# GpSimd DRAINs between the loops of every expert, and transposes inside the first product of the last block, in an attention and mixture-of-experts block

## The chip, the cores and the metric

One Trainium2 chip, one of its cores. The metric is the device time of one execution in microseconds; lower is better. The engines are TensorE (PE, with its weight loads as PEld), VectorE (DVE), ScalarE (ACT), GpSimd (POOL) and SyncE (SP). Each has its own queue of instructions, and they tell each other of progress over semaphores.

## What is computed

The reference, cut to what matters here, for 4096 tokens of 256 features:

```python
h = _layernorm(x, axis=-1) * (1 + ca) + sa
x = x + ga * _L0_attn_ref(h, w_qkv, w_out, b_out)      # linear attention, 16 heads of 64
h = _layernorm(x, axis=-1) * (1 + cb) + sb
x = x + gb * _L0_ffn_ref(h, Wg, bg, W1, b1, W2, b2)

def _L0_ffn_ref(x, Wg, bg, W1, b1, W2, b2):            # 8 experts, 2 per token, hidden size 1024
    gate_probs = jax.nn.softmax(x @ Wg + bg, axis=-1)
    _, top_idx = jax.lax.top_k(gate_probs, k)
    selected = gate_probs * expert_mask                 # expert_mask: one-hot of top_idx, summed
    selected = selected / (selected.sum(-1, keepdims=True) + 1e-08)
    h = jax.nn.gelu(jnp.einsum('bsf,efh->bseh', x, W1) + b1)
    expert_out = jnp.einsum('bseh,ehf->bsef', h, W2) + b2[None, None]
    return jnp.einsum('bsef,bse->bsf', expert_out, selected)
```

## The kernel before

The first half of the span is the attention and the routing: x1, the result of the attention, is written to `out` and, with each token's weights, to the DRAM tensor `xrows`; a list of token numbers per expert is made in `ids`. The change touches the second half, the experts.

Each expert's list is worked off in blocks of rows. `three` wide blocks of 3 x 128 rows come first, then `two` narrow ones of 2 x 128; both counts are read from registers, so each is a loop (`Fori`) on every engine. With the inputs here there are 29 blocks with 68 units of 128 rows, 10 wide and 19 narrow; the last expert has one of each, and its narrow block is the last of the program. `gv` counts the blocks. All products are made in three terms, with a high and a low part of each operand.

What each engine does in block gv:

- GpSimd. `gather` (lines 600 to 610): waits until TensorE has transposed the rows of block gv + 1 (`s_bt`), copies list entries to `gid` (line 605), and issues one indirect DMA per unit that brings rows of block gv + 2 to `listed` (line 609). `rows_of` (612 to 617): waits until all earlier scatters have landed (`s_added`) and copies the row numbers to `y_id` (616). `scatter` (619 to 626): per unit waits for VectorE's `y` and issues an indirect DMA that adds it to `out` (624). The order is gather, rows_of, scatter; in the last expert's narrow block it is rows_of, gather, scatter (lines 656 to 658).
- TensorE. `first` (1726 to 1741): 8 chunks m of the hidden layer into PSUM, 6 matmuls each. `second(gv, size, i, chunks)` (1743 to 1755): row block i of the output, 3 matmuls for each chunk of the hidden layer. `block_T(gv + 1)` (1706 to 1714): the transposes of the next block's rows, 2 per unit. It waits for VectorE's normalization (`s_norm`) and gives `s_bt`.
- ScalarE. For each of four pairs of chunks two gelus to `hid` (879) and a copy to `hid_hi` (883), then `xT_full` of the next block from the transposes (852).
- VectorE. Copies the weights to `y_w` (1403), then for each pair k `hid_lo` (1414); ahead of k = 2 it runs `take` for the next block (1350 to 1355), which waits until that block's rows have landed (`s_rows`), copies their weights to `y_next` (1353) and normalizes two units (1347); ahead of k = 3 `take_third`. Then `xT_hi` and `xT_lo` of the next block, and `y` of each row block (1425, 1426) when TensorE has given it.

At the end of the program VectorE waits for the last scatters to land and tells SP. A block ends (line 89, where the program's code stands in a context) with a DRAIN on every engine and a barrier of them all. The program's code begins with a DRAIN on every engine too (line 1802).

Of the kernel before, what the change touches and what calls it, by code (L numbers as in the profile page):

```python
# [29 lines left out]
M = FH // P  # L30
# [9 lines left out]
BI = BT // P  # L40
# [46 lines left out]
def adaln_block(nc, x, w_qkv, w_out, b_out, Wg, bg, W1, b1, W2, b2, cvec, wmod, out):  # L87
    ctx = ExitStack()
    with ctx:
# [32 lines left out]
        units = sb("units", [P, E], I32)  # L122
# [210 lines left out]
        s_blo = sem("s_blo")  # L333
# [172 lines left out]
        def _(pool):  # L506
# [125 lines left out]
            def expert(e, par, three, two, last):  # L632

                nb = three + two
                pool.reg_mov(to, e * COLS)

                def ahead(j):

                    over = j // nb
                    col = e * COLS + 2 * j + three  # L640
                    if last:
                        pool.reg_mov(at, col * (1 - over))
                    else:
                        pool.reg_mov(at, col + over * (COLS - 2 * nb - three) + j // (nb + 1))
                    return pool.snap(at, min_val=0, max_val=E * COLS - 1)

                with pool.Fori(0, three) as b:
                    gv = now(pool, g)
                    gather(ahead(b + 2), gv + 2)
                    rows_of(pool.snap(to, min_val=0, max_val=E * COLS - 3), gv, 3)  # L650
                    scatter(gv, 3)
                    pool.reg_add(to, to, 3)
                    pool.reg_add(g, g, 1)
                with pool.Fori(0, two) as b:
                    gv = now(pool, g)
                    if last:
                        rows_of(pool.snap(to, min_val=0, max_val=E * COLS - 2), gv, 2)
                        gather(ahead(three + b + 2), gv + 2, 2)
                    else:
                        gather(ahead(three + b + 2), gv + 2)  # L660
                        rows_of(pool.snap(to, min_val=0, max_val=E * COLS - 2), gv, 2)
                    scatter(gv, 2)
                    pool.reg_add(to, to, 2)
                    pool.reg_add(g, g, 1)
# [236 lines left out]
        def _(dve):  # L901
# [484 lines left out]
            def expert(e, par, three, two, last_expert):  # L1386

                def w_low_part(n):

                    dve.wait_ge(s_whi, now(dve, w) * 4 + (n + 1 + FOUR))  # L1390
                    if n < 2:
                        return dve.tensor_tensor(w1_lo[1 - par][:, n, :], w1_raw[:, n, :], w1_hi[1 - par][:, n, :].bitcast(F32), ALU.subtract)
                    m = slice((n - 2) * 4, (n - 2) * 4 + 4)
                    return dve.tensor_tensor(w2_lo[1 - par][:, m, :], w2_raw[:, m, :], w2_hi[1 - par][:, m, :].bitcast(F32), ALU.subtract)

                def rows_block(size, parts):
                    T = size * P
                    units = size if last_expert else BI
                    chain.begin()
                    gv = now(dve, g)  # L1400
                    dve.wait_ge(s_meta, gv + (1 + ONE))
                    dve.wait_ge(s_y, gv * 3 + THREE)
                    link(dve.tensor_copy(y_w[:, :, :], y_next[:, :, :]))
                    if parts:
                        w_low_part(0)
                        w_low_part(1)
                    for k in range(M // 2):
                        if k == 2:
                            take(gv + 1, units)
                        if k == 3 and units == BI:  # L1410
                            take_third()
                        dve.wait_ge(s_hidhi, gv * 4 + (k + 1))
                        m = slice(2 * k, 2 * k + 2)
                        dve.tensor_tensor(hid_lo[:, m, 0:T], hid[:, m, 0:T], hid_hi[:, m, 0:T].bitcast(F32), ALU.subtract).then_inc(s_hid, 1)  # L1414

                    if parts:
                        w_low_part(2)
                    block_parts(gv + 1, units)
                    dve.wait_ge(s_added, now(dve, wide_u if size == 3 else narrow_u) * 16 + DMA3)

                    def rows_out(i):
                        dve.wait_ge(s_f2, gv * 3 + (i + 1 + THREE))
                        bank = Y2 if i == 2 else Y0 + i
                        slot = i if size == 3 else BI + i
                        link(dve.tensor_tensor(y[:, slot, :], ps[:, bank, 0:D], b2_bc[:, e, :], ALU.add))
                        dve.scalar_tensor_tensor(y[:, slot, :], y[:, slot, :], y_w[:, i, e:e + 1], gates[:, 1, :], ALU.mult, ALU.mult).then_inc(s_y, 1 if i < size - 1 else BI - i)

                    rows_out(0)
                    if parts:
                        w_low_part(3).then_inc(s_wlo, 1)  # L1430
                        dve.reg_add(w, w, 1)
                    for i in range(1, size):
                        rows_out(i)
                    chain.end()
                    dve.reg_add(g, g, 1)
                    dve.reg_add(u, u, size)
                    dve.reg_add(got, got, units)
                    dve.reg_mov(wide_u if size == 3 else narrow_u, u)

                with dve.Fori(0, three) as b:  # L1440
                    rows_block(3, not last_expert)
                if not last_expert:
                    dve.memset(tick[:, :], 0.0).then_inc(s_wfree, 1)
                with dve.Fori(0, two) as b:
                    rows_block(2, False)
# [8 lines left out]
        def _(pe):  # L1454
# [268 lines left out]

            def expert(e, par, three, two, last_expert):

                def first(gv, size):

                    T = size * P
                    pe.wait_ge(s_blo, gv + 1)
                    for m in range(M):  # L1730
                        k = m // 2
                        if size == 3 and m in (4, 6):
                            pe.wait_ge(s_gelu, gv * 4 + (k - 1 + FOUR))
                        if m == (3 if size == 3 else 6):
                            pe.wait_ge(s_y, gv * 3 + THREE)
                        to = ps[:, k, (m % 2) * T:(m % 2 + 1) * T] if size == 2 else ps[:, m % 4, 0:T]
                        col = slice(m * P, (m + 1) * P)
                        for w_, a, st, sp_ in three_terms([((w1_hi[par][:, c, col], w1_lo[par][:, c, col]), (xT_hi[:, c, 0:T], xT_lo[:, c, 0:T])) for c in range(C)]):
                            last = pe.matmul(to, w_, a, start=st, stop=sp_)  # L1739
                        if m % 2:  # L1740
                            last.then_inc(s_f1, 1)

                def second(gv, size, i, chunks):

                    bank = Y2 if i == 2 else Y0 + i
                    if 0 in chunks and i == 2:
                        pe.wait_ge(s_gelu, gv * 4 + (M // 2 + FOUR))
                    r = slice(i * P, (i + 1) * P)
                    for m in chunks:
                        if i == 0 and m % 2 == 0:  # L1750
                            pe.wait_ge(s_hid, gv * 4 + (m // 2 + 1 + FOUR))
                        for a, w_, st, sp_ in three_terms([((hid_hi[:, m, r], hid_lo[:, m, r]), (w2_hi[par][:, m, :], w2_lo[par][:, m, :]))]):
                            last = pe.matmul(ps[:, bank, 0:D], a, w_, start=m == 0 and st, stop=m == M - 1 and sp_)  # L1753
                    if M - 1 in chunks:
                        last.then_inc(s_f2, 1 if i < size - 1 else BI - i)
# [3 lines left out]
                most, end = range(0, M - 2), range(M - 2, M)  # L1759
                with pe.Fori(0, three) as b:  # L1760
                    gv = now(pe, g)
# [9 lines left out]
                    pe.reg_add(w, w, 1)  # L1771
                with pe.Fori(0, two) as b:
                    gv = now(pe, g)
                    first(gv, 2)
                    if last_expert:
                        second(gv, 2, 0, range(0, 2))
                        block_T(gv + 1, 2)
                        second(gv, 2, 0, range(2, M))
                        second(gv, 2, 1, range(0, M))
                    else:  # L1780
                        second(gv, 2, 0, most)
                        block_T(gv + 1)
                        second(gv, 2, 1, most)
                        second(gv, 2, 0, end)
                        second(gv, 2, 1, end)
                    pe.reg_add(g, g, 1)
# [26 lines left out]
```

## Time and profile before

| | |
|---|---|
| time, median of 3 runs | 803.26 us (802.91 to 805.48) |
| time of the profiled execution | 803.23 us |
| its span, first to last instruction | 801.1 us |
| TensorE busy | 752.4 us (94%) |
| VectorE busy | 606.2 us (76%) |
| ScalarE busy | 461.5 us (58%) |
| GpSimd busy | 338.6 us (42%) |
| mean granted TensorE clock | 0.976 |

Busy times overlap and don't add up to the span. The chain that ended last is found by going back from the last instruction to what released it; what is on it sets the time. DRAINs, waits, branches and register instructions are not counted as busy. The profiled interval of an indirect DMA on GpSimd is its issue; when it has landed is told by who waits for it.

### The profile page before, as it was taken

How to read it: one execution, taken by the hardware profiler on the slowest of the kernel's cores; microseconds unless marked ns; L12 is line 12 of the kernel's file. 1: busy time of each engine (PE TensorE's matmuls, PEld its weight loads, DVE VectorE, ACT ScalarE, POOL GpSimd, SP SyncE). 2: the span in 40 equal slices, each digit the busy share in tenths (PEclk: the TensorE clock that was granted, in tenths of full speed). 3: DMA queues.
4: the chain of work that ended last, by engine and by line, in shares of the span. 5: the costliest groups of instructions: out<-in, count | busy, mean ns of one | idle time of the engine just before them, and what ended most of it. 6: DMA issues, size and time to landing. Idle time of an engine off the chain costs nothing.

```text
span 801.1 us, 16804 instructions
## 1 busy us (share of the span) xinstructions
PE 752.4 (94%) x5846; PEld 686.2 (86%) x5846; DVE 606.2 (76%) x1328; ACT 461.5 (58%) x841; POOL 338.6 (42%) x291
## 2 busy tenths in 40 slices
PE   4979999999999999976699999999999999999995
PEld 4767778788888789963599999999999999999994
DVE  6899999988898755799577767676676876876653
ACT  4465555656654542359557667574666666765643
POOL 2441413423322102400256564646556565565554
PEclk9999999999999999985799999999999999999998
DMA  8500000000000135580253532626325235233323
GB/s 286 169 1 1 1 1 1 2 1 2 1 1 2 53 106 173 171 228 5 94 146 65 145 64 42 170 43 167 54 61 145 55 83 123 49 49 60 51 56 47
DMA packets 45602, 59.58 MB, mean 74 GB/s; under 512 B 8002, under 2 KB 38788, under 8 KB 45412
## 3 DMA queue, kind: packets, MB, share of 16 engines
q0 software_dynamic: 14352, 21.85, 15.0%
q1 hardware_dynamic: 31188, 36.93, 14.5%
q8 instruction: 36, 0.59, 0.3%
q14 instruction: 26, 0.21, 0.1%
HBM read 40.49 MB, written 18.27 MB: 73 GB/s over the span
## 4 chain that ended last, share of the span: by engine, by line
PE 74%; DVE 16%; issue 5%; ACT 2%; DMA 1%; POOL 1%; POOLq 0%; DVEq 0%; SPq 0%; ACTq 0%
PE ps L1739 23%; PE ps L1753 23%; PE ps L1539 7%; PE ps L1497 7%; PE ps L1564 3%; PE ps L1713 2%; PE ps L1548 2%; PE ps L1636 2%; DVE q_max L966 2%; DVE q_sum L973 2%; DVE k_blk L1076 2%; DVE q_exp L967 1%; ACT at_lo L814 1%; DVE ln_s L930 1%; PE ps L1618 1%
## 5 line engine op out<-in xcount | busy, mean ns | idle before, releaser
L879 ACT ACTIVATE hid<-ps,b_col 128x256 f32<-128x256 f32 (+1 forms) x232 | 105.6, 507 | 113.9 <-PE ps L1739 111.0
L1753 PE MATMUL ps<-w_hi,hid_hi 128*128 128x256 f32 x544 | 154.4, 284 | 0.0
L1753 PE MATMUL ps<-w_hi,hid_lo 128*128 128x256 f32 x544 | 151.9, 279 | 0.0
L1753 PE MATMUL ps<-w_lo,hid_hi 128*128 128x256 f32 x544 | 151.9, 279 | 0.0
L1414 DVE TENSOR_TENSOR hid_lo<-hid,hid_hi 128x512 fp32r<-128x512 f32 (+1 forms) x116 | 90.9, 784 | 73.4 <-ACT hid_hi L883 73.3
L1739 PE MATMUL ps<-xT_hi,w_hi 128*128 128x256 f32 (+1 forms) x464 | 139.6, 301 | 1.6 <-DVE xT_lo L1366 1.6
L1739 PE MATMUL ps<-xT_lo,w_hi 128*128 128x256 f32 (+1 forms) x464 | 139.5, 301 | 0.0
L1739 PE MATMUL ps<-xT_hi,w_lo 128*128 128x256 f32 (+1 forms) x464 | 139.4, 300 | 0.0
L624 POOL DMA_INDIRECT out<-y,y_id x68 | 117.3, 1725 | 39.5 <-POOL y_id L616 16.6
L545 POOL TENSOR_TENSOR q_n<-q_exp,q_rec 128x1024 f32<-128x1024 f32 (+1 forms) x33 | 61.0, 1851 | 172.5 <-DVE q_rec L974 172.5
L609 POOL DMA_INDIRECT listed<-xrows,gid x86 | 94.2, 1096 | 42.0 <-POOL gid L605 24.6
L1753 PEld LDWEIGHTS ps<-w_hi,hid_hi 128*128 128x128 f32 x544 | 102.3, 188 | 0.0
L1753 PEld LDWEIGHTS ps<-w_lo,hid_hi 128*128 128x128 f32 x544 | 102.3, 188 | 0.0
L1753 PEld LDWEIGHTS ps<-w_hi,hid_lo 128*128 128x128 f32 x544 | 102.2, 188 | 0.0
L1497 PE MATMUL ps<-wqk_hi,h_q 128*128 128x512 f32 x248 | 92.6, 416 | 1.6 <-DVE q_exp L967 1.4
L1739 PEld LDWEIGHTS ps<-xT_hi,w_hi 128*128 128x128 f32 x464 | 88.1, 190 | 2.0 <-DVE xT_lo L1366 2.0
L712 ACT ACTIVATE k_exp<-ps,k_new 128x512 f32<-128x512 f32 x64 | 44.0, 687 | 77.8 <-DVE k_new L1077 76.4
L1739 PEld LDWEIGHTS ps<-xT_lo,w_hi 128*128 128x128 f32 x464 | 87.9, 189 | 0.0
L1739 PEld LDWEIGHTS ps<-xT_hi,w_lo 128*128 128x128 f32 x464 | 87.8, 189 | 0.0
L883 ACT ACTIVATE hid_hi<-hid 128x512 fp32r<-128x512 f32 (+1 forms) x116 | 82.0, 707 | 3.7
L1539 PE MATMUL ps<-h_q,wqk_hi 128*128 128x512 f32 x256 | 80.3, 395 | 0.0
L1076 DVE TENSOR_REDUCE k_blk<-ps 128x1 f32<-128x512 f32 x64 | 43.4, 678 | 19.8 <-PE ps L1539 19.4
(215 smaller groups left out, 1454.0 us busy)
## 6 DMA issues: line engine op xcount, KB each, us to landing
w_raw<-in_L_ffn_W SPq DMA_DIRECT2D x16, 1024.0 KB
x_all<-in_L_attn_x SPq DMA_DIRECT2D x8, 512.0 KB, 9.3
out<-x_all SPq DMA_DIRECT2D x8, 512.0 KB, 3.0
xrows<-x_all SPq DMA_DIRECT2D x8, 512.0 KB, 4.5
listed<-xrows,gid POOLq DMA_INDIRECT x86
out<-y,y_id POOLq DMA_INDIRECT x68
wqk_raw<-in_L_attn_w_qkv SPq DMA_DIRECT2D x2, 512.0 KB, 6.4
wqk_raw<-in_L_attn_w_qkv SPq DMA_DIRECT2D x1, 1024.0 KB, 10.5
```

What stands on the lines that cost most here:

```text
L545: ins = pool.tensor_tensor(q_n[:, s % 2, i, :].rearrange("p (h d) -> p h d", d=DH)[:, hs, :], q_exp[:, i % 2, :].rearrange("p (h d) -> p h ...
L609: pool.indirect_dma_start(listed[:, i, :], None, xrows[:, :], bass.IndirectOffsetOnAxis(ap=gid[:, i:i + 1], axis=0)).then_inc(s_rows, 16)
L624: pool.indirect_dma_start(out[:, :], bass.IndirectOffsetOnAxis(ap=y_id[:, i:i + 1], axis=0), y[:, i if size == 3 else BI + i, :], None, co ...
L712: act.activation(k_exp[:, n % 2, :], ps[:, KT + n % 2, :], ACT.Exp, bias=k_new[:, s % 2, j:j + 1]).then_inc(s_ke, 1)
L879: ins = act.activation(hid[:, m, 0:T], src, ACT.Gelu_apprx_tanh, bias=b1_col[:, e, m:m + 1])
L883: act.activation(hid_hi[:, m, 0:T], hid[:, m, 0:T], ACT.Copy).then_inc(s_hidhi, 1)
L1076: link(dve.tensor_reduce(k_blk[:, j:j + 1], ps[:, KT + n % 2, :], AX, ALU.max, negate=True))
L1414: dve.tensor_tensor(hid_lo[:, m, 0:T], hid[:, m, 0:T], hid_hi[:, m, 0:T].bitcast(F32), ALU.subtract).then_inc(s_hid, 1)
L1497: last = pe.matmul(ps[:, b + half, :], a, w, start=st, stop=sp_)
L1539: last = pe.matmul(ps[:, KT + n % 2, :], w, a, start=st, stop=sp_)
L1739: last = pe.matmul(to, w_, a, start=st, stop=sp_)
L1753: last = pe.matmul(ps[:, bank, 0:D], a, w_, start=m == 0 and st, stop=m == M - 1 and sp_)
```

## The change

GpSimd gets a DRAIN behind the loop of wide blocks of each of the eight experts. In the last expert's narrow blocks VectorE takes the next block's rows ahead of the first pair (k = 0) instead of the third, TensorE makes the next block's transposes behind 5 of the 8 chunks of the first product instead of behind 2 chunks of the second, and the second product does 6 chunks of row block 0, 2 of row block 1, the last 2 of row block 0 and the last 6 of row block 1.

```diff
@@ GpSimd, expert
                     scatter(gv, 3)
                     pool.reg_add(to, to, 3)
                     pool.reg_add(g, g, 1)
+                pool.drain()
                 with pool.Fori(0, two) as b:
@@ VectorE, rows_block
                     for k in range(M // 2):
-                        if k == 2:
+                        if k == (2 if units == BI else 0):
                             take(gv + 1, units)
@@ TensorE, expert
-                def first(gv, size):
+                def first(gv, size, ms=range(M)):

                     T = size * P
-                    pe.wait_ge(s_blo, gv + 1)
-                    for m in range(M):
+                    if 0 in ms:
+                        pe.wait_ge(s_blo, gv + 1)
+                    for m in ms:
@@ TensorE, narrow blocks
                     gv = now(pe, g)
-                    first(gv, 2)
                     if last_expert:
-                        second(gv, 2, 0, range(0, 2))
+                        first(gv, 2, range(0, M - 3))
                         block_T(gv + 1, 2)
-                        second(gv, 2, 0, range(2, M))
-                        second(gv, 2, 1, range(0, M))
+                        first(gv, 2, range(M - 3, M))
+                        second(gv, 2, 0, most)
+                        second(gv, 2, 1, range(0, 2))
+                        second(gv, 2, 0, end)
+                        second(gv, 2, 1, range(2, M))
                     else:
+                        first(gv, 2)
                         second(gv, 2, 0, most)
```

`units` is 2 in the last expert's narrow blocks alone, `BI` is 3, `M` is 8, `most` is chunks 0 to 5 and `end` chunks 6 and 7.

In TensorE's queue, before, the end of the first product and the start of the second in the last narrow block (line 1739 is the first product, 1753 the second, 1713 the transposes):

```order
L1739 MATMUL ps<-xT_lo,w_hi 128x256
L1739 MATMUL ps<-xT_hi,w_lo 128x256
L1751 ISA
L1753 MATMUL ps<-w_hi,hid_hi 128x256
L1753 MATMUL ps<-w_lo,hid_hi 128x256
L1753 MATMUL ps<-w_hi,hid_lo 128x256
L1753 MATMUL ps<-w_hi,hid_hi 128x256
L1753 MATMUL ps<-w_lo,hid_hi 128x256
L1753 MATMUL ps<-w_hi,hid_lo 128x256
L1708 ISA
L1713 MATMUL ps<-ident,listed 128x128 x4
```

The transposes stand behind two chunks of the second product. After, the piece around them (lines are up to two higher: 1741, 1714):

```order
L1741 MATMUL ps<-xT_hi,w_hi 128x256
L1741 MATMUL ps<-xT_lo,w_hi 128x256
L1741 MATMUL ps<-xT_hi,w_lo 128x256
L1709 ISA
L1714 MATMUL ps<-ident,listed 128x128 x4
L1741 MATMUL ps<-xT_hi,w_hi 128x256
L1741 MATMUL ps<-xT_lo,w_hi 128x256
L1741 MATMUL ps<-xT_hi,w_lo 128x256
```

They now stand inside the first product, with three of its chunks behind them.

In VectorE's queue, the same block before:

```order
L1403 COPY y_w<-y_next 128x24
L65 REGISTER_ALU
L1412 ISA
L1414 TENSOR_TENSOR hid_lo<-hid,hid_hi 128x2x256
L1412 REGISTER_ALU
L1414 TENSOR_TENSOR hid_lo<-hid,hid_hi 128x2x256
L421 ISA
L1353 COPY y_next<-listed 128x24
L1347 TENSOR_SCALAR listed<-listed 128x256 x2
```

And after:

```order
L1404 COPY y_w<-y_next 128x24
L65 REGISTER_ALU
L421 ISA
L1354 COPY y_next<-listed 128x24
L1348 TENSOR_SCALAR listed<-listed 128x256 x2
L1413 ISA
L1415 TENSOR_TENSOR hid_lo<-hid,hid_hi 128x2x256
```

The take has moved ahead of all four hid_lo. GpSimd's queue is the same but for the DRAINs, which such a listing leaves out.

## Rows read from the trace of the kernel before

**Rows 1.** The page: span, and the chain that ended last, by engine.
```profile
span 801.1 us, 16804 instructions
...
PE 74%; DVE 16%; issue 5%; ACT 2%; DMA 1%; POOL 1%; POOLq 0%; DVEq 0%; SPq 0%; ACTq 0%
```

**Rows 2.** The chain of waits, 490 to 545 us: start us, us, what.
```profile
503.16 5.65 PE ps L1739 x48
508.81 2.12 PE ps L1753 x18
510.93 0.66 PE ps L1713 x6
...
```

**Rows 3.** The chain of waits, 740 us to the end.
```profile
783.48 3.76 DMA out<-y,y_id
...
787.49 0.20 POOL y_id L616
...
793.11 2.64 POOLq L89
```

**Rows 4.** Line 89: engine, operation, ns min/median/max, first and last start us.
```profile
L89 POOLq DRAIN  x1: 7792/7792/7792, 793.1 to 793.1; - x1
...
L89 DVEq DRAIN  x1: 17/17/17, 798.2 to 798.2; - x1
L89 SPq DRAIN  x1: 7/7/7, 798.3 to 798.3; - x1
```

**Rows 5.** GpSimd's timeline, last row: start us, us, engine, line, operation.
```profile
794.18 1.57 POOL L624 DMA_INDIRECT out<-y,y_id  x1 [0.30 <-issue]
```

**Rows 6.** One stretch: busy us of PE, PEld, DVE, ACT, POOL; clock, DMA share, GB/s.
```profile
798.00:799.00 1.00, 0.00 (x0) 0.00 (x0) 0.00 (x0) 0.00 (x0) 0.00 (x0) 0.50 0.00 0
```

**Rows 7.** Line 1802, where the program begins: columns as in rows 4.
```profile
L1802 POOLq DRAIN  x1: 183/183/183, 0.4 to 0.4; - x1
```

**Rows 8.** DMA issues by line: out<-in, queue, operation, count, median us to landing.
```profile
listed<-xrows,gid POOLq DMA_INDIRECT x86
out<-y,y_id POOLq DMA_INDIRECT x68
...
listed<-xrows,ids POOLq DMA_INDIRECT x6, 2.8
```

**Rows 9.** GpSimd's timeline from the third expert's wide to its narrow blocks.
```profile
508.58 1.55 POOL L624 DMA_INDIRECT out<-y,y_id  x1 [0.30 <-DVE y_next L1353]
511.83 0.19 POOL L605 COPY gid<-ids 128x3 int32 x1 [1.70 <-PE ps L1713]
...
515.78 0.96 POOL L609 DMA_INDIRECT listed<-xrows,gid  x1 [0.30 <-issue]
```

**Rows 10.** VectorE's and TensorE's timelines in the narrow block after that.
```profile
519.93 0.17 DVE L1353 COPY y_next<-listed 128x24 f32<-128x24 f32 x1
520.02 0.73 DVE L1347 TENSOR_SCALAR listed<-listed 128x256 f32<-128x256 f32 x2
520.71 0.69 DVE L1414 TENSOR_TENSOR hid_lo<-hid,hid_hi 128x512 fp32r<-128x512 f32 x1
...
521.69 0.28 PE L1753 MATMUL ps<-w_hi,hid_hi 128*128 128x256 f32 x1
```

**Rows 11.** Timelines of GpSimd, VectorE and TensorE around the last block.
```profile
777.34 0.95 POOL L609 DMA_INDIRECT listed<-xrows,gid  x1 [0.30 <-issue]
...
782.49 0.69 DVE L1414 TENSOR_TENSOR hid_lo<-hid,hid_hi 128x512 fp32r<-128x512 f32 x1 [1.58 <-ACT hid_hi L883]
...
786.74 0.69 DVE L1414 TENSOR_TENSOR hid_lo<-hid,hid_hi 128x512 fp32r<-128x512 f32 x1 [0.72 <-ACT hid_hi L883]
...
791.86 0.48 DVE L1426 SCALAR_TENSOR_TENSOR y<-y,y_w,gates 128x256 f32<-128x256 f32 x1
...
785.71 0.60 PE L1713 MATMUL ps<-ident,listed 128*128 128x128 f32 x4
...
787.56 0.31 PE L1753 MATMUL ps<-w_hi,hid_hi 128*128 128x256 f32 x1
```

## The prediction

> **What bounds the kernel now.** Three views, in this order: the page for the whole, the chain of waits for the expert stage and the end, and the answers on single lines for the DRAINs and the last block. The page gives a span of 801.1 us and a chain that is 74% TensorE and 1% GpSimd [rows 1]. In the expert stage that chain holds TensorE alone: first product, second product, transposes, second product, back to back [rows 2]. So an edit on GpSimd or VectorE there costs or gains nothing until TensorE has to wait for it. In the last 18 us the chain leaves TensorE and runs over GpSimd: the third scatter of the wide block lands 3.76 us after its start, at 787.24, the copy to y_id follows at 787.49, then two gathers, two scatters, and line 89 [rows 3]. Line 89 is the end of the block, and there GpSimd has a DRAIN. It starts at 793.1 and lasts 7.792 us, so to 800.9; SP's and VectorE's are over at 798.3 [rows 4]. The last scatter of the program holds GpSimd from 794.18 to 795.75 [rows 5]; with the 3.76 us of [rows 3] it lands at 797.94, and from 798 on the DMA engines are idle [rows 6]. The DRAIN therefore ends 5.15 us after GpSimd's last instruction and 3.0 us after the last landing. As nothing else lasts beyond 798.3, 2.6 us of the span are this DRAIN alone.
>
> **What a DRAIN costs.** Before has two on GpSimd. The one at the start, with no DMA behind it, lasts 183 ns [rows 7]. The one at the end has 160 indirect DMAs behind it (86 + 68 + 6) [rows 8]. Two readings fit both. (i) It goes through the DMAs issued since the last DRAIN one by one: 5.15 us / 160 = 0.032 us each, and it can't end before the last has landed. (ii) It waits for the last landing and then takes a fixed 3.0 us. No row decides; a new DRAIN is bounded by 0.18 us from below and by landing plus 3.0 us from above. I take (i): in the 3 us after the landing there is no transfer that a fixed wait could be for, and with nothing outstanding the price is not paid.
>
> **The DRAINs with more experts behind them, seven of the eight.** The third expert's is typical. The third scatter of its wide block starts at 508.58 and is issued by 510.13; the next copy to gid waits until 511.83 [rows 9] for the transposes, whose piece of the chain ends at 511.59 [rows 2]. The scatter lands at 508.58 + 3.76 = 512.34. A DRAIN that ends there, plus 0.5 us, puts the copy to gid at 512.8, 1.0 us late. The 0.5 us are twice the 0.25 us between landing and copy in [rows 3]: once until the DRAIN's end is noticed, once for branch, registers and waits, which ran ahead before. Queued behind it on GpSimd are three gathers, the last starting at 515.78 [rows 9], a copy to y_id and two scatters. Who waits: VectorE's take in the next block, at 519.93 [rows 10]. With 2.8 us to landing [rows 8] the rows are there at 518.6, 1.35 us ahead. Beyond the take there is 0.3 us more: hid_lo of the third pair ends at 521.40, TensorE wants it at 521.69 [rows 10]. That is 1.6 us of cover against 1.0 us of lateness: cost 0, with 0.6 us left. If the cover is gone, the third hid_lo is late next, then the transposes. By (i) the counting is covered as well: at most about 26 DMAs lie between two DRAINs, 26 x 0.032 = 0.8 us after 510.13.
>
> **The DRAIN in the last expert.** The third scatter lands at 787.24, and the copy to y_id waits for that anyway [rows 3]; the counting of 26 DMAs is over before. Added are the same 0.5 us (bounds 0 and, by (ii), 3.5). Behind it stand everything that ends the kernel, two gathers and two scatters, and they move as a whole: VectorE's last y is done at 792.34 [rows 11], and its scatter starts only at 794.18 [rows 5].
>
> **The DRAIN at the end.** By (i) four DMAs are left to it, it ends with the last landing, and what stands at 798.3 becomes the end: -2.6 us. By (ii) 0.
>
> **Take, transposes and second product in the last expert's narrow block.** There is one such block, the last of the program. TensorE has the same 96 matmuls and 4 transposes in another order. Transposes cost 0.66 us for six [rows 2], so 0.44 us for these four. They now stand ahead of the second half of the third pair instead of behind the second product's first two chunks, so gelu, hid_hi and hid_lo of the last two pairs come 0.44 us later: hid_lo of the fourth ends at 787.87 instead of 787.43 [rows 11]. TensorE wants it after 18 matmuls more than stood ahead of the transposes before (785.71 [rows 11]), at 2.12 us for 18 [rows 2]: 785.71 + 0.44 + 2.12 = 788.27. The two chunks of the second row block that are put in between give that room; before, TensorE's matmul there showed 0.31 instead of 0.28 us [rows 11]. Its end stays where it is. Take now stands in the 1.58 us in which VectorE is idle ahead of the first hid_lo, from 780.91 to 782.49; its rows land at 777.34 + 2.8 to 3.8 = 780.1 to 781.1 [rows 11], and copy and two normalizations take 0.9 us [rows 10], so it ends at 782.0 at the latest. GpSimd's gather in this block stands behind the copy to y_id, so earlier transposes release nothing. Cost 0, under the 1.8 us of cover of the last y. One risk: the fourth hid_lo now runs beside GpSimd's copy to y_id and could stretch it by 0.2 to 0.4 us.
>
> **Sum.** The profiled execution took 803.23 us (span 801.1 and 2.1 around it), the median is 803.26; the sum stands for both. 803.2 + 0 (seven DRAINs) + 0.5 (the eighth) - 2.6 (the end) + 0 (the block) = **801.1 us**. About 0.3%, 2.4 us, is what a measurement of this kernel can tell from no change; the forecast lies just inside that.
>
> **Rivals.** *A DRAIN is light, and the end keeps its tail.* The new ones wait for GpSimd's own instructions, 0.2 us, and what is slow at the end belongs to the end. For it: SP's and VectorE's DRAINs last 7 and 17 ns [rows 4]. Against it: on GpSimd it is the same instruction in both places. Time: 803.2, up to 803.8 with stretched copies. The Trainium skill (VectorE: DVE Perf Modes, "The DRAIN you can't avoid") calls the DRAINs that the runtime puts on all five engines constant, about 12 ns; by that rule this rival holds and the time is 803.2. SP's and VectorE's rows agree with it, GpSimd's 183 and 7792 ns do not.
>
> *A DRAIN is slow every time.* Reading (ii), landing plus 3.0 us. In seven experts the gathers come 4.0 us late against 1.6 us of cover, and TensorE stands 2.4 us each, 16.8 us. In the last expert y_id comes 3.5 us late, and the end keeps its tail. Time: 803.2 + 16.8 + 3.5 = 823.5. It decides from the point where a DRAIN ends more than 0.6 us after the landing. For it: the 3.0 us behind the last landing, which no row ties to a number of DMAs. Against it: a fixed time of that length has no work to be seen in.
>
> *Between them*, a fixed 1 us after each landing: 7 x 0.4 + 1.5 - 2.0 = +2.3, so 805.5.
>
> **How the numbers follow.** DMAs counted one by one (801.1, own range 800.5 to 801.9): 0.57. Light DRAIN: 0.23. Slow: 0.18. Between: 0.02. The range runs from 800.5 (the eighth DRAIN free, 803.2 - 2.6, rounded down) to 804.2 (light DRAINs, copies stretched in every block) and leaves out the last two, 0.20. Faster by over 0.3% needs more than 2.4 us, the lower end of the likeliest case: 0.15. Slower: the last two, 0.20. Same: 0.65.
>
> **What would show it.** Right: ten DRAINs of GpSimd, the eight new ones ending with the landing of the scatter ahead of them; the last ending near 798.6; the last block's copy to y_id near 788.0; TensorE without idle time in the expert stage. Light: the new ones end with the third scatter, and the last still ends 5 us behind GpSimd. Slow: TensorE waits some 2 us in the second narrow block of every expert. The prediction is wrong if TensorE's waits in that stage add up to over 1 us, or if the last DRAIN ends over 1 us after the last landing.

## The result, and the profile after

| | before | changed |
|---|---|---|
| time, median | 803.09 us (801.89 to 805.48, 4 runs) | 830.73 us (828.7 to 832.0, 4 runs) |
| ratio, 95% interval | | 1.034 [1.030, 1.037] |
| span of the profiled execution | 801.1 us | 829.9 us |
| mean granted TensorE clock | 0.976 | 0.959 |

The change costs 27.6 us, where 801.1 us was forecast and 804.2 us was the end of the range. The page of the changed kernel shows at once that the chain is another one. Span and shares of the chain by engine (before: [rows 1]):

```profile
span 829.9 us, 16812 instructions
...
PE 53%; DVE 19%; issue 14%; POOL 4%; POOLq 3%; DMA 3%; ACT 3%; DVEq 0%; SPq 0%; ACTq 0%
```

TensorE's share has gone from 74% to 53%, and POOLq, GpSimd's sequencer with the DRAINs in it, has 3%. The next view is that of TensorE's waits from 390 us to 830 us (what waited, for whom: us in total, times, longest):

```profile
PE ps L1755 <- DVE hid_lo L1415: 19.4, 7, 3.7
PE ps L1741 <- DVE xT_lo L1367: 1.6, 1, 1.6
```

The second line is there before too, with the same 1.6 us; the first is new. Seven times the second product waits for `hid_lo`, once in each of experts 1 to 7: 3.65, 3.41, 3.66, 3.49, 2.60 and 2.28 us, and only 0.3 us in expert 7. The DRAINs, before the narrow loops and at line 89, with their ns (shortest, median, longest; before: [rows 4]):

```profile
L654 POOLq DRAIN  x8: 6610/9928/10841, 411.1 to 811.5; - x8
```

```profile
L89 POOLq DRAIN  x1: 6445/6445/6445, 823.1 to 823.1; - x1
L89 DVEq DRAIN  x1: 17/17/17, 829.6 to 829.6; - x1
L89 SPq DRAIN  x1: 7/7/7, 829.7 to 829.7; - x1
```

The one at the end is over at 829.5, before VectorE's: its tail of 2.6 us is gone, as forecast. The longest of line 654 is the third expert's:

```profile
L654 POOLq DRAIN  x1: 10841/10841/10841, 516.6 to 516.6; - x1
```

A DRAIN stands in its sequencer ahead of its time, beside the scatters that are still being issued (it starts at 516.55, the last scatter before it only at 519.54), so its length is no cost. Its end is: 516.55 + 10.84 = 527.39. GpSimd's timeline there answers to [rows 9]:

```profile
515.36 1.63 POOL L624 DMA_INDIRECT out<-y,y_id  x1 [0.92 <-DVE y L1427]
517.29 1.95 POOL L624 DMA_INDIRECT out<-y,y_id  x1 [0.30 <-issue]
519.54 1.55 POOL L624 DMA_INDIRECT out<-y,y_id  x1 [0.30 <-issue]
528.51 0.19 POOL L605 COPY gid<-ids 128x3 int32 x1 [7.41 <-issue]
529.55 1.03 POOL L609 DMA_INDIRECT listed<-xrows,gid  x1 [0.86 <-POOL gid L605]
```

From the end of the third scatter's issue to the copy to `gid` it is 7.41 us, before 1.70 us [rows 9]: the copy is **5.7 us late**, where 1.0 us was forecast. The chain of waits carries that on to TensorE:

```profile
521.09 6.33 issue
...
530.88 0.98 POOL listed L609
...
532.17 2.80 DMA listed<-xrows,gid
534.97 0.02 issue
534.99 0.06 DVE y_next L1354
...
535.82 0.61 DVE hid_lo L1415
536.42 0.04 issue
536.47 1.65 PE ps L1755 x6
```

The 6.33 us are the DRAIN. Then come the gathers, the landing of the rows (2.80 us), VectorE's take, and behind the take in VectorE's queue the `hid_lo` for which TensorE waits. This is the way that the prediction drew; only TensorE had 3.66 us to wait at its end:

```profile
536.47 0.58 PE L1755 MATMUL ps<-w_hi,hid_hi 128*128 128x256 f32 x1 [3.66 <-DVE hid_lo L1415]
536.85 0.41 PE L1755 MATMUL ps<-w_lo,hid_hi 128*128 128x256 f32 x1
```

And the matmuls behind the wait last 0.41 us in place of 0.28 us. The stretches around it show why (us; busy us of PE, PEld, DVE, ACT, POOL, with the number of instructions; clock, DMA share, GB/s):

```profile
530.00:534.00 4.00, 2.81 (x25) 2.60 (x23) 0.69 (x1) 2.96 (x7) 2.71 (x4) 1.00 0.31 80
534.00:538.00 4.00, 1.53 (x7) 1.53 (x8) 2.35 (x6) 0.00 (x0) 3.31 (x2) 0.73 0.36 55
538.00:542.00 4.00, 4.00 (x21) 4.00 (x20) 1.75 (x4) 2.56 (x4) 1.49 (x2) 0.50 0.29 33
542.00:546.00 4.00, 4.00 (x28) 4.00 (x28) 1.86 (x5) 0.56 (x1) 2.46 (x4) 0.91 0.37 102
```

Before, the same piece of the work ran at full clock, 37 matmuls in 4 us:

```profile
522.00:526.00 4.00, 4.00 (x37) 4.00 (x35) 2.44 (x5) 2.82 (x5) 1.50 (x2) 1.00 0.30 33
```

From about the end of the wait TensorE is granted half its clock, 1.2 GHz, here for 6.8 us (535.9 to 542.7), and from 538 to 542 it does 21 matmuls. The same is seen around the end of four of the other five long waits, for 3.4 or 6.8 us; behind the sixth expert's, 2.28 us long, the clock stays full. Before, the clock is full from 394 to 796 us. The whole stage, after and before:

```profile
390.00:830.00 440.00, 411.90 (x3196) 410.26 (x3195) 277.50 (x555) 250.34 (x441) 234.04 (x215) 0.97 0.36 78
```

```profile
390.00:801.00 411.00, 401.29 (x3196) 401.08 (x3194) 278.12 (x555) 249.86 (x441) 235.94 (x215) 0.99 0.39 83
```

**The books.** The same 3196 matmuls are 10.6 us longer (411.90 − 401.29). With 19.4 us of waits, and 1.2 us less from TensorE's last matmul to the end of the span (8.6 us, before 9.8 us), that makes 28.8 us, and the spans differ by 28.8. The clock accounts for the 10.6 us: the five stretches at half clock are 23.8 us long, 2.4 us of them are still waits, and half of the rest is 10.7 us.

### The profile page after: what moved, and what is told of

Same layout as the page of the kernel before. It is cut to its first block, busy times and chain, and to the rows that moved or that the text cites. A ratio compares the mean times of both kernels' runs of the same rounds, so it can differ in the third digit from the quotient of the medians.

```text
span 829.9 us, 16812 instructions
## 1 busy us (share of the span) xinstructions
PE 764.5 (92%) x5846; PEld 696.6 (84%) x5846; DVE 605.8 (73%) x1328; ACT 461.8 (56%) x841; POOL 336.5 (41%) x291
## 4 chain that ended last, share of the span: by engine, by line
PE 53%; DVE 19%; issue 14%; POOL 4%; POOLq 3%; DMA 3%; ACT 3%; DVEq 0%; SPq 0%; ACTq 0%
PE ps L1741 14%; PE ps L1755 13%; PE ps L1540 7%; PE ps L1498 6%; PE ps L1565 3%; DMA listed<-xrows,gid 2%; PE ps L1549 2%; POOLq L654 2%; PE ps L1637 2%; DVE q_max L967 2%; POOL listed L609 2%; POOL out L624 2%; PE ps L1714 2%; DVE q_sum L974 2%; DVE k_blk L1077 2%
## 5 line engine op out<-in xcount | busy, mean ns | idle before, releaser
L1755 PE MATMUL ps<-w_hi,hid_hi 128*128 128x256 f32 x544 | 158.6, 291 | 19.4 <-DVE hid_lo L1415 19.4
L1755 PE MATMUL ps<-w_lo,hid_hi 128*128 128x256 f32 x544 | 154.6, 284 | 0.0
L1755 PE MATMUL ps<-w_hi,hid_lo 128*128 128x256 f32 x544 | 154.4, 284 | 0.0
L1755 PEld LDWEIGHTS ps<-w_hi,hid_hi 128*128 128x128 f32 x544 | 105.5, 194 | 20.8 <-DVE hid_lo L1415 20.8
L1755 PEld LDWEIGHTS ps<-w_lo,hid_hi 128*128 128x128 f32 x544 | 105.7, 194 | 0.0
L1755 PEld LDWEIGHTS ps<-w_hi,hid_lo 128*128 128x128 f32 x544 | 105.2, 193 | 0.0
L853 ACT ACTIVATE xT_full<-ps,modc 128x384 f32<-128x384 f32 (+1 forms) x58 | 35.4, 660 | 49.5 <-PE ps L1714 49.5
## 6 DMA issues: line engine op xcount, KB each, us to landing
wqk_raw<-in_L_attn_w_qkv SPq DMA_DIRECT2D x1, 1024.0 KB, 10.6
```

The source lines that it names most:

```text
L853: act.activation(xT_full[:, c, 0:units * P], ps[:, XTB + c, 0:units * P], ACT.Identity, bias=modc[:, 2, c:c + 1], scale=modc[:, 3, c:c + 1 ...
```

## Where the 5.7 us came from

The forecast had the third scatter land 2.2 us after its issue (512.34 in before's time). It lands 5.4 us after it, and **it was as late before the change** (5.1 us): by the DMA records in the trace of the kernel before, the scatters that stand ahead of the first narrow block of experts 1 to 6 land 4.4 to 5.35 us after their issue, and those elsewhere 2.1 to 2.6 us. Nobody waited for them there, so no chain showed it. Two views of the kernel before did, and the prediction used neither. The first is SyncE's timeline, the second DMA shares around the scatter at 508.58:

```profile
504.34 0.37 SPq L462 DMA_DIRECT2D w_raw<-in_L_ffn_W  x1
504.75 0.47 SPq L463 DMA_DIRECT2D w_raw<-in_L_ffn_W  x1
```

```profile
508.00:510.00 2.00, 2.00 (x19) 2.00 (x19) 1.99 (x6) 1.94 (x5) 1.70 (x2) 1.00 1.03 329
510.00:512.00 2.00, 2.00 (x20) 2.00 (x20) 0.69 (x1) 0.73 (x2) 0.30 (x2) 1.00 1.11 312
512.00:514.00 2.00, 2.00 (x20) 2.00 (x19) 1.60 (x4) 0.86 (x2) 1.15 (x2) 1.00 1.10 217
514.00:516.00 2.00, 2.00 (x20) 2.00 (x19) 1.66 (x5) 0.00 (x0) 1.39 (x3) 1.00 0.28 72
```

When VectorE is through with an expert's wide blocks, it releases SyncE, which starts the loads of a later expert's weights, two of 1 MB. They fill all DMA engines (a share of 1.03 to 1.11 at 217 to 329 GB/s) until about 514, and the scatter shares them. Each DRAIN stands just behind that scatter. For experts 7 and 8 there is nothing left to load; the changed kernel's wait in expert 7 is 0.3 us, against 2.28 to 3.66 us in the six with a load. It was the scatter of the last expert, with 3.76 us from the start, that the prediction took for all.

So there are three suspects for the lateness: the landing, what the DRAIN does behind it, and the way from the DRAIN's end to the copy. And a rival for the whole: the new order in the last block, or something in the DRAIN beyond the place where it stands.

## The experiments

**1. The DRAINs alone, and the order alone.** The kernel before with each half of the change.

```diff
@@ GpSimd, expert, before's kernel
                     pool.reg_add(g, g, 1)
+                pool.drain()
                 with pool.Fori(0, two) as b:
```

> The eight DRAINs without the new order of the last block. Theory A (the loss is the DRAINs, through TensorE's waits and the clock that they cost): within 1 us of the changed kernel, 830 us, and TensorE waits again some 19 us for hid_lo in seven experts. Rival B (the new order of the last block takes a part of the loss): below 829 by that part. If the order is worth nothing, the two kernels differ by under 1 us.

Measured: 835.2 us (832.7 to 836.2), ratio 1.040 [1.037, 1.042].

```profile
PE ps L1754 <- DVE hid_lo L1415: 21.2, 7, 3.7
```

> The new order of take, transposes and second product in the last block, without DRAINs. Theory A: the end is set by GpSimd, whose chain (landing of the third scatter, y_id, two gathers, two scatters) is untouched, so 803.1 within 0.4 us. Rival B: the order costs time, over 804. A third possibility, a gain, would need GpSimd's last scatter to start earlier than 3.2 us ahead of the last landing, and nothing in the order gives that.

Measured: 803.42 us (801.8 to 805.9), ratio 1.001 [0.999, 1.002], no wait of the second product. Its last DRAIN has its whole tail again:

```profile
L89 POOLq DRAIN  x1: 8180/8180/8180, 791.3 to 791.3; - x1
...
L89 DVEq DRAIN  x1: 17/17/17, 796.8 to 796.8; - x1
```

The DRAINs make all of the loss, and the reordered block by itself costs nothing, as forecast. That the DRAINs alone stand 4.5 us above the whole change, where 1 us was expected at most, raised the question whether the order gives something back.

**2. The changed kernel once more**, unchanged.

> The changed kernel once more, beside the others on one chip, for its difference to the kernel with the DRAINs alone (830.7 and 835.2 in two measurements). If the new order gives 4.5 us back, this is at 830.7 again; if the two differ by the scatter of how long TensorE waits and how the clock answers, it lies anywhere from 829 to 836.

Measured: 831.9 us (827.3 to 835.1), ratio 1.034 [1.031, 1.038]; its profiled execution has a span of 833.0 us and waits of 19.6 us, with 1.6 us more of waits in the DRAINs-only kernel. The profiled spans overlap (829.9 and 833.0 against 832.7). By the medians 3.1 to 4.5 us lie between the two kernels, by the ratios 4.5 to 4.9 us, and no view explains them. In experiments 1 and 6 the order moves nothing; whether it gives something back beside DRAINs between the loops stays open.

**3. DRAINs at two places.** Behind the wide blocks of the second and of the last expert alone.

```diff
@@ GpSimd, expert, before's kernel
                     pool.reg_add(g, g, 1)
+                if e in (1, E - 1):
+                    pool.drain()
                 with pool.Fori(0, two) as b:
```

> DRAINs behind the wide blocks of experts 2 and 8 alone, with about 31 and 128 DMAs behind them. It asks how the time after the landing grows with the number. Straight line through the changed kernel's eight (0.04 us + 0.0425 us each): 1.4 us for the first, 5.5 us for the second. Line with a ceiling near 69 DMAs (as the 2.98 us after 163 DMAs at the end of before would have it): 1.4 and 3.0. Counting alongside from the end of the last issue (0.032 us each): the second ends 4.1 us after the last issue, 1.9 us after the landing. The time: TensorE waits in one expert instead of seven, so about 4 us, and the end gives 2.6 back while the eighth DRAIN costs its 3 to 5.5 us: 807 to 811.

Measured: 807.94 us, ratio 1.006 [1.004, 1.009] (2 runs); TensorE waits once, 3.9 us, in the second expert. The last expert has no load and no wait. So one DRAIN beside a load costs some 5 us, about a seventh of the loss. The second expert's DRAIN, with 31 DMAs behind it, ends 1.32 us after the last landing, as expected (1.4). The last expert's, with 128, ends only 0.71 us after; all three readings of the expectation, 5.5, 3.0 and 1.9 us, were too high.

**4. Small loads.** If the loads make the landing late, DRAINs beside small loads must cost much less. Of the weights of experts 3 to 8 only columns 0 to 7 are loaded (the rest of those experts' weights is left out, and everything else runs as it did), without and with the eight DRAINs.

```diff
@@ SyncE, before's kernel
-                load_weights(e)
+                sp.dma_start(w1_raw[:, :, 0:8], W1[e, :, 0:8].rearrange("(c p) n -> p c n", p=P)).then_inc(s_w1raw, 16)
+                sp.dma_start(w2_raw[:, :, 0:8], W2[e, :, 0:8].rearrange("(m p) n -> p m n", p=P)).then_inc(s_w2raw, 16)
```

> Before, but of the weights of experts 3 to 8 only 8 columns are loaded (24 KB per expert or so instead of 2 MB), so the output of those experts is not the reference's; all matmuls and waits stay. It is the base for the next kernel. TensorE bounds the stage and never waits for weights, so 803 within 1 us.

> The same small loads with the eight DRAINs behind the wide blocks. Theory A says that six of the DRAINs are long because the scatter ahead of them shares the DMA engines with 2 MB of weights (it lands 4.4 to 5.7 us after its issue, against 2.2 in experts 7 and 8). With small loads (experts 3 to 8; the loads of experts 1 and 2 are issued earlier) the landings of all are 2.2 us after the issue, a DRAIN ends 3.1 us after it, the copy to gid comes 4.2 us after it instead of 1.7, 2.5 us late against some 1.6 to 2.0 of cover: TensorE waits 0.5 to 1 us in seven experts, as in expert 7 of the kernel with DRAINs alone (0.84), 4 to 7 us in all, and the clock falls less or not: 806 to 810 against small loads without DRAINs at 803. Rival D (the landing is late because the DRAIN itself holds it up): the landings stay at 5 us and the time at 830 or more.

Measured: 802.58 us without DRAINs, ratio 1.000 [0.999, 1.001], and 809.07 us with them, ratio 1.009 [1.007, 1.011]. Waits of the second product, and the third expert's DRAIN in GpSimd's timeline, in the second kernel:

```profile
PE ps L1755 <- DVE hid_lo L1416: 3.2, 5, 1.2
```

```profile
509.05 1.55 POOL L625 DMA_INDIRECT out<-y,y_id  x1 [0.30 <-issue]
514.79 0.18 POOL L606 COPY gid<-ids 128x3 int32 x1 [4.19 <-issue]
```

The same 21 DMAs stand behind the same DRAIN, and it ends 3.1 us after the issue (with loads 6.3 us). The copy is 4.19 − 1.70 = 2.5 us late, and no wait is over 1.2 us. (The longest is the fourth expert's, where the scatter lands 3.5 us after its issue even so, and not 2.1 to 2.3 as in the others.) So the loads themselves cost nothing (802.58), and the DRAINs beside small ones 6.5 us. Beside full ones they cost 29.0 us in the changed kernel (831.9 against 802.87, same chip) and 32.1 in the DRAINs-only kernel. **22 to 26 us of the loss need the loads.** The remaining 6.5 us also show that the forecast would have been wrong without them: 2.5 us late, not 1.0.

**5. A plain wait in each DRAIN's place.** GpSimd waits there until all earlier scatters have landed, and does nothing else.

```diff
@@ GpSimd, expert, before's kernel
                     pool.reg_add(g, g, 1)
+                pool.wait_ge(s_added, now(pool, u) * 16 + DMA3)
+                pool.sem_inc(s_turn_pool, 1)
                 with pool.Fori(0, two) as b:
```

> Before, with a wait in the place of each DRAIN: GpSimd waits until all scatters up to there have landed, as rows_of does, and goes on. It parts the wait for the landing from the DRAIN's own work (0.7 to 1.1 us behind the landing, and some 1.1 us from its end to the next copy). Theory A: the copy to gid then comes 0.3 us behind the landing, so 5.2 + 0.3 = 5.5 us behind the issue instead of 7.4, 1.9 us earlier; TensorE waits some 1.6 us instead of 3.5 in the experts that load weights, nothing in experts 7 and 8: 10 us of waits instead of 20, and with less of the half clock 812 to 818. If the DRAIN's own work were all of the loss, 803; if none of it, 830. The last DRAIN stays at 3 us behind the landing.

Measured: 827.89 us (826.6 to 828.2), ratio 1.031 [1.029, 1.033]. The expectation was too low by 10 us and more: **the wait for the landing, with the way from there to the copy, brings most of the loss** (25.0 of 29.0 us), with no DRAIN in the kernel but those of before. Its waits, its chain and GpSimd's timeline in the third expert:

```profile
PE ps L1755 <- DVE hid_lo L1416: 16.0, 7, 3.6
```

```profile
517.46 6.79 DMA out<-y,y_id
524.79 0.25 POOLq L644
525.68 0.80 issue
526.47 0.78 POOL listed L609
```

```profile
517.46 1.55 POOL L624 DMA_INDIRECT out<-y,y_id  x1 [0.30 <-issue]
525.44 0.19 POOL L605 COPY gid<-ids 128x3 int32 x1 [6.42 <-issue]
```

The first line of the chain is the number that the prediction needed: 6.79 us from the start of this scatter to its landing, where it had 3.76 [rows 3]. The copy comes 525.44 − 524.25 = 1.2 us after the landing. That is a way behind any halt at this place: the loop's branch, and the registers for the list's position (POOLq L644), which ran ahead before. With a DRAIN it is 0.9 us from landing to the DRAIN's end and 1.1 us from there to the copy. Against the changed kernel it has 3.4 us less of waits (16.0) and 2.3 us less of TensorE's busy time (409.6 us in the stage), but 1.6 us more from TensorE's last matmul to the end (10.2 against 8.6 us), since its last DRAIN has its tail back: 4.1 us in sum. The profiled spans, 829.9 and 825.8 us, are 4.1 us apart, the medians on the same chip 4.0. The DRAINs-only kernel, with this one's order, is 7 us above it (1.040), more by what experiment 2 left unexplained.

**6. The DRAINs behind the narrow loops.** There GpSimd has no work in hand until TensorE's next transposes, and no DRAIN stands in front of a gather that someone needs soon.

```diff
@@ GpSimd, expert
                     pool.reg_add(to, to, 2)
                     pool.reg_add(g, g, 1)
+                if not last:
+                    pool.drain()
```

> Before, with seven DRAINs in another place: behind the loop of narrow blocks of experts 1 to 7, so ahead of the next expert's wide block, where GpSimd is idle for 4.8 us; the last block's order as before. Theory A (a DRAIN ends at the last landing plus about 0.04 us for each DMA since the last DRAIN): the scatter ahead has no weight load beside it and lands some 2.2 us after its issue, 15 to 26 DMAs take 0.7 to 1.2 us, the sequencer 1.1 us more, in all 4.0 to 4.5 us after the issue, against about 4.8 us of idle time. TensorE waits for nothing, and the last DRAIN has 10 DMAs behind it instead of 163, so that it ends with SP's: 803.1 - 2.5 = 800.6 us. Rival C (a DRAIN costs a fixed time that only shows when it is slow, and the end's tail belongs to the end): 803.1 or more, and the last DRAIN still ends 3 us after the last landing.

> The kernel before with a DRAIN behind the narrow loops of experts 1 to 7, once more, beside the run above. If its gain of 2 us is real, 800.2 to 801.5 us, ratio 0.996 to 0.999 with an interval below 1; if it was scatter, 802.5 to 803.5.

> The changed kernel's order in the last block, with the seven DRAINs behind the narrow loops of experts 1 to 7 instead of the eight between the loops. If all of the loss comes from where the DRAINs stand, this is as fast as the kernel before with the moved DRAINs, 800.4 to 801.4 us, with no wait of TensorE over 1 us in the expert stage. If the reordered last block adds something once GpSimd's lists are short, it differs from that kernel by over 0.5 us.

Measured:

| kernel | time, us | ratio to before |
|---|---|---|
| before's order, moved DRAINs | 800.87 (800.1 to 801.7) | 0.9975 [0.9964, 0.9986] |
| the same again | 800.73 (800.3 to 800.9) | 0.9972 [0.9961, 0.9983] |
| the changed kernel's order, moved DRAINs | 800.47 (799.8 to 802.0) | 0.9971 [0.9961, 0.9982] |

Seven DRAINs in the right place make the kernel 2.2 to 2.5 us **faster than before** by the medians, a small gain, but the interval lies below 1 all three times. The last of the three kernels, its DRAINs and GpSimd's timeline across the DRAIN at 530.05:

```profile
L666 POOLq DRAIN  x7: 6017/6263/6564, 436.2 to 765.5; - x7
```

```profile
531.52 1.73 POOL L624 DMA_INDIRECT out<-y,y_id  x1 [0.30 <-issue]
538.12 1.20 POOL L605 COPY gid<-ids 128x3 int32 x1 [4.86 <-PE ps L1715]
```

```profile
L89 POOLq DRAIN  x1: 5787/5787/5787, 793.1 to 793.1; - x1
...
L89 DVEq DRAIN  x1: 17/17/17, 798.7 to 798.7; - x1
```

That DRAIN is over at 530.05 + 6.05 = 536.1, and the copy is still released by TensorE's transposes (PE ps), with the 4.86 us of idle time that it has without any DRAIN. The one at line 89 has 10 DMAs left and ends at 798.9, with VectorE's. From the start of the last scatter to the end of the span it is 4.5 us, before 6.9 us: this is the whole gain. The order of the last block makes no difference here either, 800.47 against 800.73.

**7. How a DRAIN counts.** Two DRAINs, behind the narrow loops of experts 2 and 5 (`if e in (1, 4)` in the diff above).

> Two DRAINs only, behind the narrow loops of experts 2 and 5: 46 and 53 indirect DMAs stand before them, 64 before the one at the end. By 0.04 us and 0.0425 us for each DMA since the last DRAIN they end 2.0, 2.3 and 2.8 us after the last landing before them. If the price stops growing at some number between 32 and 64, they end 1.4 us after it. Time: the end keeps a tail of about the same length as before (before: 3.0 us), so 802.5 to 803.2.

Measured: 803.47 us (800.9 to 804.0), ratio 1.000 [0.999, 1.001]; the three DRAINs end 1.93, 2.24 and 2.97 us after the last landing (expected: 2.0, 2.3 and 2.8). The tail at the end is that of before:

```profile
L89 POOLq DRAIN  x1: 8290/8290/8290, 792.5 to 792.5; - x1
...
L89 DVEq DRAIN  x1: 17/17/17, 798.1 to 798.1; - x1
```

With all kernels together, from the traces' DMA records, GpSimd's DMAs since the last DRAIN (163 are all of a program, 3 of them not indirect) and time from the last landing to the DRAIN's end:

| DMAs | 4 | 10 | 16 | 21 | 26 | 32 | 46 | 53 | 64 | 128 | 163 |
|---|---|---|---|---|---|---|---|---|---|---|---|
| us | 0.21 | 0.45 | 0.70 | 0.90 | 1.11 | 1.35 | 1.93 | 2.24 | 2.97 | 0.71 | 2.98 |

Up to 53 the points lie within 0.07 us of 0.04 + 0.0425 per DMA; at 64 it is 0.2 us more. The counting runs **behind** the last landing. It doesn't go by the time since the last DRAIN: the changed kernel's first, 421 us after the one at the start and with 15 DMAs behind it, ends 0.67 us after the landing, its second, 47 us later with 16, 0.70 us after. Nearly every DMA here moves 128 rows, so whether it goes by DMAs or by rows no run tells; "per DMA" stands for both. The two large numbers are off the line. The 0.71 us of 128 are what 16 cost, and the 2.98 us of 163 what 64 cost, so something must take DMAs off the list in between. That is argued from two numbers; what does it, and at which number, stays open, and no run was made for it.

## Why the prediction was wrong

**"The scatter lands at 508.58 + 3.76 = 512.34": this is the step that failed.** It took the landing of the last expert's scatter for that of the third expert's. Beside the weight loads it is 6.79 us from the start (experiment 5), and 5.4 in place of 2.2 us from the end of the issue in the changed kernel: +3.2 us. The number was never on the chain, and only in the last expert does anybody wait for such a scatter.

**"Counting is covered as well: at most 26 DMAs."** The kind of the cost was right, reading (i) with its price per DMA, and the fixed 3.0 us of reading (ii) fell: with 4 DMAs the rest is 0.21 us. But the prediction let the counting run beside the landing, from the issue on. It runs behind it: +0.9 us with 21 DMAs. The price, 0.032 us, was the tail since the issue by all 160 DMAs; it is 0.0425 us, of fewer.

**"Plus 0.5 us" to the copy.** From the DRAIN's end to the copy it is 1.1 us, +0.6, also taken from the last expert (0.48 us there in the changed kernel), whose narrow loop begins with `rows_of` and not with the gather and its registers. In the third expert all three together make 1.0 + 3.2 + 0.9 + 0.6 = 5.7 us, which is what the timeline shows.

**"1.6 us of cover."** About right: 5.7 us of lateness left 3.66 us of waiting, so 2.0 us were covered. Who waits for whom was right too, from the copy over gathers and take to `hid_lo`. "Cost 0, with 0.6 us left" had no room for a landing that was taken from one place.

**The clock stood in no term.** TensorE is granted half its clock around the end of five of the six long waits, which brings 10.6 us more of busy time beside 19.4 us of waits. The slow rival, "TensorE stands 2.4 us each, 16.8 us", priced the waits alone as well. It had the place, the seven waits and nearly their size right; with 10.6 us for the clock, and without the 2.6 us of tail that did go, its 823.5 us would have been 831.5. That would have been luck, as the reason is another one: the landing, not a fixed 3.0 us.

**The eighth DRAIN and the end.** "+0.5" and "−2.6", −2.1 in sum; measured −1.2 from TensorE's last matmul on. The tail did go. The last expert's copy to `y_id` comes 3.8 us after the last issue, in place of 2.4, since 26 DMAs take 1.1 us behind the landing, and the last scatter starts 825.57 − 822.33 = 3.2 us after VectorE's last `y`, before 1.8 us [rows 5, 11].

**"Take, transposes and second product: cost 0."** Right, by the order alone (1.001) and beside moved DRAINs (800.47 against 800.73 us); beside DRAINs between the loops it stays open (experiment 2).

**The light DRAIN**, which the prediction gave 0.23, fell everywhere. The Trainium skill (VectorE: DVE Perf Modes, "The DRAIN you can't avoid") has the DRAINs that the runtime puts around a program at about 12 ns on all five engines. Those at line 89 belong to the program itself; VectorE's 17 and SyncE's 7 ns are near that figure, and GpSimd's is not, with 6445 ns even where only 4 DMAs stand behind it.

The signs that the prediction named told the truth: waits of TensorE in the stage that "add up to over 1 us" were 19.4 us. That the last DRAIN would end with the last landing held to 0.2 us.

## What to carry to other kernels

A halt on GpSimd behind indirect DMAs costs their landing, then 0.04 us for each DMA since the last DRAIN if it is a DRAIN (measured up to 53), and then about 1 us until the next work starts. Put it where the queue is idle anyway; there seven of them gained 2.2 to 2.5 us, by a shorter list for the DRAIN at the end. Take a landing time only from a place with the same transfers beside it: when nobody waits for a DMA, the chain doesn't show it, and the DMA share of that stretch and the queue of the loads must be read instead. And price a new wait of TensorE with the clock behind it: here each us of waiting cost on average half a us more (10.6 for 19.4, and 8.3 for 16.0 with the plain wait). For a single wait that is no rule: one of 3.60 us in the kernel with the plain wait left the clock full.

## What the runs showed of the hardware

- A DRAIN of GpSimd takes 0.18 us with no DMA behind it. Else it ends 0.2 us (4 DMAs) to 2.97 us (64) after the last landing, and off that line 0.71 us (128) and 2.98 us (163) after.
- An indirect scatter that adds lands 2.1 to 2.9 us after its issue where no weights are loaded (one beside the small loads: 3.5 us), and 4.4 to 5.8 us after it beside loads of 2 MB.
- Around the end of waits of 2.3 to 3.7 us TensorE's granted clock mostly fell to 0.50, for 3.4 to 6.8 us: five times of six in the changed kernel, four of six in the one with the plain wait. There a wait of 3.60 us (until 579.85) and one of 2.18 us were followed by full clock. Around waits of up to 1.2 us (small loads) the stage's clock stayed at 0.99 (before: 0.99), and TensorE's busy time was 2.9 us above that with small loads alone; why, stays open.
